# One transfer for the inverses of a half, a new order of SyncE's transfers, weights spread over 16 batches, and slot counting in batch 15

## What is computed

```
def _L0_xattn_ref(q, k, v):          # 8 heads of 16 features, 512 x 512 scores each
    qk = jnp.einsum('bdm,bdn->bmn', qh, kh) * scale
    sm = jax.nn.softmax(qk, axis=-1)
    ret = jnp.einsum('bmn,bcn->bcm', sm, vh)
def _L0_ffn_ref(x, wg, W, b):
    probs = softmax(xt @ wg); idx = argmax(probs); gate = probs[idx]
    out = gate * (W[idx] @ xt + b[idx])
x = x + tanh(g_xattn) * _L0_xattn_ref(_layernorm(x), ctx, ctx)
x = x + tanh(g_ffn) * _L0_ffn_ref(_layernorm(x), wg, W, b)
```

## Time and profile before

| what | value |
|---|---|
| time, median of 3 runs | 586.75 us (580.72, 586.75, 587.75) |
| time of the profiled execution, and its span | 586.23 us, 584.6 us |
| TensorE busy | 515.4 us (88%) |
| VectorE busy | 422.7 us (72%) |
| ScalarE, GpSimd busy | 349.7 us, 352.5 us (60% each) |
| mean granted TensorE clock | 0.977 |
| chain that ended last, largest line | PE L1420 (the experts' products), 10% |
| transfers | 50392 packets, 90.90 MB |

### The profile page before, as it was taken

How to read it: one execution, slowest core, us unless ns; L and a number is a source line. 1 busy time by engine, 2 the same in 40 slices (tenths; PEclk the granted TensorE clock), 3 DMA queues, 4 the chain that set the end, 5 groups by cost and what they waited for, 6 DMA issues and landing times. The chain is left out here.

```text
span 584.6 us, 9983 instructions
## 1 busy us (share of the span) xinstructions
PE 515.4 (88%) x2603; PEld 183.0 (31%) x2603; DVE 422.7 (72%) x831; ACT 349.7 (60%) x429; POOL 352.5 (60%) x568
## 2 busy tenths in 40 slices
PE   0389999889887999998999999998979979899994
PEld 0012323222323232323333232323322235355551
DVE  5898988768785789888999998989998565112121
ACT  3217887758684778786887877886855842111110
POOL 7444478756564657685767777885473446544532
PEclk9999999989997899999999999999997999999998
DMA  4875457666666486776557555545540154643410
GB/s 141 237 154 178 140 174 201 217 176 185 185 191 176 131 229 197 197 205 175 161 162 213 166 171 153 165 127 158 127 116 24 38 181 163 186 138 98 127 55 0
DMA packets 50392, 90.90 MB, mean 156 GB/s; under 512 B 22018, under 2 KB 24066, under 8 KB 50320
## 3 DMA queue, kind: packets, MB, share of 16 engines
q1 hardware_dynamic: 36096, 65.28, 40.9%
q0 software_dynamic: 10560, 24.93, 12.9%
q10 hardware_dynamic: 3696, 0.23, 0.4%
HBM read 66.91 MB, written 28.41 MB: 163 GB/s over the span
## 5 line engine op out<-in xcount | busy, mean ns | idle before, releaser
L948 DVE TENSOR_REDUCE neg_max<-ps_ring 128x1 f32<-128x512 f32 x480 | 309.0, 682 | 48.9 <-PE ps_ring L1315 47.6
L852 ACT ACTIVATE probs<-ps_scores 128x1024 f32<-128x1024 f32 x256 | 250.1, 1022 | 75.0 <-PE ps_scores L1334 74.2
L1315 PE MATMUL ps_ring<-stacks 96*128 96x512 bf16 x480 | 171.2, 393 | 14.8 <-DVE neg_max L948 13.7
L1334 PE MATMUL ps_scores<-stacks 128*128 128x512 bf16 x512 | 157.1, 390 | 14.9 <-DMA stacks<-shift_parts 8.5
L1357 PE MATMUL ps_pv<-probs,v_ones 128*32 128x512 f32 x992 | 135.2, 618 | 0.0
L1315 PEld LDWEIGHTS ps_ring<-stacks 96*128 96x128 bf16 x480 | 47.1, 98 | 171.4 <-DVE neg_max L948 125.1
L1420 PE MATMUL ps_scores<-w_sb,f_xt 128*128 x184 | 83.2, 593 | 0.0
L1334 PEld LDWEIGHTS ps_scores<-stacks 128*128 128x128 bf16 x512 | 48.2, 102 | 70.4 <-ACT probs L852 21.6
L836 ACT COPY f_xt<-ps_scores 128x512 f32<-128x512 f32 x23 | 13.5, 586 | 72.2 <-PE ps_scores L1401 72.2
L605 POOL CAST shift_parts<-shift 16x128 bf16<-16x128 f32 x32 | 9.0, 282 | 64.6 <-DVE shift L955 64.3
L1420 PEld LDWEIGHTS ps_scores<-w_sb,f_xt 128*128 128x128 f32 x184 | 34.5, 190 | 33.0 <-issue 32.2
(11 more groups left out here) (149 smaller groups left out, 499.8 us busy)
## 6 DMA issues: line engine op xcount, KB each, us to landing
stacks<-parts_dram SPq DMA_DIRECT2D x224, 64.0 KB, 3.0
parts_dram<-prep POOLq DMA_DIRECT2D x15, 768.0 KB, 5.4
w_sb<-w_t SPq DMA_DIRECT2D x16, 512.0 KB, 4.9
recs_dram<-rec SPq DMA_DIRECT2D x16, 512.0 KB, 3.2
stacks<-parts_dram SPq DMA_DIRECT2D x32, 192.0 KB, 3.4
prep<-x_perm SPq DMA_DIRECT2D x16, 256.0 KB, 2.9
prep<-k_perm SPq DMA_DIRECT2D x16, 256.0 KB, 3.2
v_in<-v_t SPq DMA_DIRECT2D x16, 256.0 KB, 3.3
```

The costliest lines, as they stand in the source:

```text
L852: nc.scalar.activation(probs[:, k % 2, 2 * jp:2 * jp + 2], ps_scores[:, jp], ACT.Exp).then_inc(exp_done, 1)
L948: nc.vector.tensor_reduce(neg_max[:, g, j, c:c + 1], ps_ring[:, SLOT[tile]], AX.X, ALU.max, negate=True).then_inc(ring_free, 1)
L1315: nc.tensor.matmul(ps_ring[:, SLOT[tile]], q_stack[0:KS, into.p, g, j, c * 128:(c + 1) * 128], k_stack[0:KS, into.p, g, j], start=True, st ...
L1334: last = nc.tensor.matmul(ps_scores[:, jp, j % 2], k_stack[0:KA, B.p, g, j, c * 128:(c + 1) * 128], q_stack[0:KA, B.p, g, j], start=True, ...
```

## The change

`spread_recips` becomes one transfer for a half: it writes all 128 partitions of `scale[:, g]` (256 KB instead of four times 32 KB), and for that `recip_dram` gets a second row for each head, which a new transfer in batch 0 sets to zero. `store_recips` writes its rows two apart. On SP, the store of half 0 goes ahead of the rows and keys, and its spread goes behind the stacks of half 1 and the values. The weights come in 16 pieces, one in each batch. `count_tiles(0)`, `find_blocks(0)` and `read_slots(0)` move to batch 15, `take_columns(0)` goes behind `find_gates(2)`, and `number_places(1)` with its four transfers goes behind `rstd2` in batch 14.

```diff
-                sp.dma_start(recip_dram[g].rearrange("j (t c) -> (j t) c", c=DM // 32), sums[:, g]).then_inc(recips_out[g], 16)
+                sp.dma_start(recip_dram[g, :, g].rearrange("j (t c) -> j t c", c=DM // 32), sums[:, g]).then_inc(recips_out[g], 16)
...
-                for j in range(NJ):
-                    at = 32 * j + g * DH
-                    sp.dma_start(scale[at:at + DH, g], recip_dram[g, j].partition_broadcast(DH)).then_inc(recips_in[g], 16)
+                sp.dma_start(scale[:, g], recip_dram[g].rearrange("j h m -> (j h) m").unsqueeze(1).to_broadcast([NJ * 2, DH, DM])
+                             ).then_inc(recips_in[g], 16)
...
-                for piece in range(2):
-                    sp.dma_start(w_sb[:].rearrange("p c e n -> p (c e n)")[:, bass.ds(B.b * (2 * n) + piece * n, n)],
-                                 w_t[bass.ds(B.b * 2 + piece, 1)].rearrange("o p n -> (o p) n")).then_inc(w_loaded, 16)
+                sp.dma_start(w_sb[:].rearrange("p c e n -> p (c e n)")[:, bass.ds(B.b * n, n)],
+                             w_t[bass.ds(B.b, 1)].rearrange("o p n -> (o p) n")).then_inc(w_loaded, 16)
...
-                if not isinstance(B.b, int) or B.b < NB // 2:
-                    load_weights(B)
+                load_weights(B)
...
                 if B.known(0):
                     sp.wait_ge(dve_const, DVE_CONSTS)
+                    sp.dma_start(recip_dram.rearrange("g j h m -> (g j h) m"), scale[0:NG * NJ * 2, 0]).then_inc(recip_cleared, 16)
...
+                if by_transfer(B):
+                    store_recips(B, 0)
                 if not isinstance(B.b, int) or B.b + 4 < NB:
                     load_rows_keys(B.plus(4))
-                if by_transfer(B):
-                    store_recips(B, 0)
-                    spread_recips(B, 0)
                 if stack:
                     load_stack(B.plus(2), 1)
                     load_values(B.plus(2))
+                if by_transfer(B):
+                    spread_recips(B, 0)
...
                 split_maxima(B, 1)
                 load_shift(B, 1)
+                read_slots(0)
                 spread_sums(B.plus(-1), 1)
...
-                if B.known(RANKED[1]):
-                    number_places(1)
-                    store_tokens(*GROUPS[1])
                 if prev:
                     add_high(B.plus(-1))
                 split_maxima(B.plus(1), 0)
                 if prev:
                     rstd2(B.plus(-1))
+                if B.known(RANKED[1]):
+                    number_places(1)
+                    store_tokens(*GROUPS[1])
...
-                if B.known(RANKED[1]):
-                    read_slots(0)
...
                 take_maxima(B, ring_base(B) + 1, 1, SLOT["turn1"])
+                count_tiles(0)
+                find_blocks(0)
                 turn_sums(B.plus(-1), 1)
                 invert_sums(B.plus(-1), 1)
-                take_columns(0)
...
                 find_gates(2)
+                take_columns(0)
                 add_attention(B.plus(-1))
...
-                        if B.known(RANKED[1]):
-                            if at == (2, 2):
-                                count_tiles(0)
-                            if at == (3, 2):
-                                find_blocks(0)
```

More of the change, by code:

```diff
@@ L259, in build @@
         consts_in = sem("consts_in")
+        recip_cleared = sem("recip_cleared")
         table_set = sem("table_set")
```

10 lines of the change are left out of this document (6 added, 4 removed).

## The result

The changed kernel takes 579.26 us in the median, the kernel before 585.95 (16 executions each); the ratio is 0.989, 95% interval 0.987 to 0.992. That is 6 us faster, which is within the 2% that count as the same, and less than half of the 14.7 us forecast. The ratio and its interval leave out slow executions, among them one of the changed kernel at 2775.8 us; the medians are over all.

The account below looks back on a forecast made before the run. With no engine full, it took transfer waits and half clock in batches 2 to 7, and counting in batch 14, as the loss: -12.0 - 1.5 - 5.5 + 1.5 + 2.8 = -14.7 from 586.23, so 571.5 us; 80% range 561 to 583.

Parts of the forecast that it names:

- a term of 1.5 of their own: Weights leaving batches 0 to 7: batches 6 and 7 gain 1.5 us of their 2.5 us excess; later batches pay 0.
- The single spread: One spread per half: high inverse later in quiet batches, taken as 0.2 us in each of 14 batches, 2.8 in all.
- Does the high inverse arrive earlier?: Step on the high half's landing: spread at 4.0 us, 0.9 later than now, store 0.3 later, so 1.2 later.
- The issue gain: SP's queue, half 1: one spread issue of about 0.43 us instead of four taking 1.73, so 1.3 us less.
- Rival 3: Few engines make the high inverse late in each of 14 batches: 16.8 us instead of 2.8, total 585.5; chance 0.11.
- 2 us of slack, cost nothing: Low inverse, read in batch 9: spread lands at 322.7, `add_low` begins at 324.74, so no cost.
- Batch 15: Thirteen counting instructions take 2.7 us, 0.9 late, and `take_columns(0)` adds 0.5 ahead of `add_attention(14)`: cost 1.5 us.
- rival 2: New half clock in batch 15, behind TensorE's idling ahead of 469.99: 6.8 us lost in the experts, total 578; chance 0.17.
- Batch 14: Without the counting on VectorE it becomes a quiet batch with its places and gates: 5.5 of 6.35 us gained.
- Batches 2 to 5: Shift issued earlier by SP clears batches 3 to 5, not 2: 12.0 of 16.0 us of waits and half clock gained.
- The store: High inverse's store in its new 4 x 32 x 16 form: taken as 0.3 us later, bounds 0 and 2.7.
- rival 4: Rows and keys land late, stalling VectorE's statistics at each batch's head: 32 us at a landing of 8, 604; chance 0.07.

Follow-up runs that it names:

- e3: The kernel before with only the four spreads of a half made one transfer and the store written to every second row: 595.6 us, ratio 1.020.
- e5: The changed kernel with the four spreads of 32 KB per half back in place of the single one: 569.6 us, ratio 0.974 to the kernel before.
- e10: The changed kernel with four spreads again, those of half 0 issued between the query and key stacks of half 1: 559.9 us, ratio 0.959 to the kernel before.
- e1: The kernel before with only the slot counting and the POOL steps that belong to it moved to batch 15: 577.0 us, ratio 0.993.
- e13: The kernel before with each inverse stored twice and one spread of 256 KB on 16 engines: 575.7 us, ratio 0.979.
- e15: The changed kernel with four spreads, half 0's directly behind rows and keys, and the counting behind `find_experts(2)`: 556.8 us, ratio 0.952 to the kernel before.
- e18: The kernel before with early store, four spreads behind rows and keys, weights over 16 batches, counting behind `find_experts(2)`, old store form: 554.06 us, ratio 0.952.

## Why the prediction was wrong

Two steps failed: it priced the single spread by its own landing alone, at 2.8 us where it costs 11.7 alone, and it took the low inverse to have 2 us of slack, where its lateness costs some 9.7. A third, that SP is one stall's cause and not the bound, hid what order and weights bring.

- **What bounds the kernel.** The prediction said that no engine is full and counted the shift waits and half clock of batches 2 to 5 as the prize. It did read SP's store as 3.8 us late, but took SP as one stall's cause, not as the bound of the stage. The round of 28.64 us, in the same trace, would have told: every microsecond off SP's list was a microsecond of the batch, until 25.45. Order and weights are worth 8.3 and 8.5 us alone, and the weights, with a term of 1.5 of their own and an unpriced share of the 12.0, were the worst undersized.
- **The single spread (+2.8, the issues counted as gain).** The step that failed is "Does the high inverse arrive earlier?": it priced the landing of the spread itself and nobody else's. Engines and packets were read rightly, 8 and 4; in e3 the price was VectorE's wait for the sums, a transfer on four engines. Measured alone: +11.7 us (7.4 to 15.9); in the changed kernel, by e5, 8.4, by a way that is in part open. The issue gain was oversized too: one spread takes 0.62 to 0.67 us of issue, not 0.43, and the store 0.25 more than before, which leaves some 0.8 of the 1.3 us. Rival 3 had the cause, few engines, with a cost of 16.8 us at another wait. It had 0.11.
- **The low inverse ("2 us of slack, cost nothing").** It costs 9.7 us (e5 to e10). In batch 9 the spread went out 1.6 us later than forecast, counted from the inversion (the stacks' issue, 5.5 us for 4), and landed 6.0 instead of 2.9 us later; these 4.7 us, less the slack of 2, are the wait of 3.00 but for 0.3. I had two landings, 2.9 and 4.0, and used the upper one only for the high half. Both were read from transfers with little in front; this one has 0.75 MB of stacks and 256 KB of values ahead of it.
- **Batch 15 (+1.5, measured +4.8).** The mechanism was right, the size not: thirteen instructions in 3.9 us for 2.7, and then half clock. That is rival 2, at another gap than the one it named. Alone (e1) the term was right, +1.3, and in e10 with full clock +1.9.
- **Batch 14 (-5.5):** the size was right, -6.5, and -7.3 in e1, the reading not: half of the 5.4 us read as counting were two instructions slowed beside POOL's products, and e3 and e13 lose most of this stall with the counting in place. The counting as a whole was forecast at -4.0 and measured at -4.1; with the stages of e1 at -7.3 and +1.3, so close a fit is in part luck.
- **Batches 2 to 5 (-12.0):** the shift waits left as said; the stage gained 8.7, since the waits behind the low inverse and the sums came in.
- **The store ("0.3 later"):** true where nothing stands in its way (SP stands 1.43 us behind it at the least in e15, 1.12 in e18), with 0.25 us more of issue, and harmless in the new order. In the old one it costs 10 to 13 us.
- **Rows and keys (rival 4), and the weights' upper bound of 7.5:** did not happen. VectorE's waits for `prep` are 1.9 us, as before.

The sum of the parts alone (-9) lies between forecast and result. The forecast's -14.7 would have been about right without the single spread, e5 gives 569.6, but by luck: what order and weights brought above their terms, the late low inverse took back.

## What to carry over

Before you price a stall, read the issuing queue's timeline over one whole round: if it never stands except for its own transfers, that queue is the bound there, and each wait and issue on it counts in full until the next bound; after that, nothing. Do this for every stage: here it held from batch 2 to 4 and no further. When small instructions are slow beside their like, look at what other engines do in that time. Merging transfers saves issues, but ask on how many engines the merged one runs and which small, urgent transfers use the same ones. Price a late landing by what is queued ahead of it, not by the median of its kind.

## What was not expected of the hardware

- One transfer of 256 KB on 8 engines against the same bytes on 16, at the same place in the queue: 595.6 against 575.7 us for the whole kernel, 28 transfers in all, so 0.7 us for each.
- An 8 KB transfer that lands 9.2 us after its issue, with stacks and weights around it; 7.3 in the kernel before.
- Two VectorE instructions on 8 numbers and on 1 number a partition that take 1.95 and 1.18 us beside products of POOL, and 0.17 and 0.22 without, in six kernels alike.
- Effects do not add over a bound: the new store costs 12.7 us in one order and nothing in the other, and the parts that gain 4.1, 8.3 and 8.5 alone give 28 together in e18 (by its ratio), where the spread and the counting also have better places.
